# Five groups in the first tile list, tiles beside the last attention step, and 128 streamed columns in gates, values and logits

## What is computed

```python
q, k, v = layernorm(x), ctx, ctx                      # 32 x 128 x 256, 4 heads of 64
g = concat([q, k, v]) @ gate_kernel + bias            # input and forget gate of each head
cs = cumsum(log_sigmoid(fg)); log_D = tril(cs_i - cs_j) + ig_j
D = exp(log_D - max_j log_D); C = (q k^T / 8) * D
h = C / (max(|sum_j C|, exp(-max log_D)) + 1e-6) @ v
x = x + head_layernorm(h) * scale
n = layernorm(x); p = softmax(n @ router^T)           # 4096 tokens x 8 experts
top 2 of p, weights normalised
x = x + sum over the 2 experts e of w_e * (gelu(n @ w1[e]) @ w2[e])   # 256 -> 1024 -> 256
```

## Time and profile before

| | |
|---|---|
| median of 3 runs | 709.69 us |
| the profiled execution | 706.96 us, span of its instructions 705.2 us |
| PE matmul busy | 617.1 us (88%), 5872 records |
| PE weight load busy | 503.1 us (71%) |
| DVE, ACT, POOL busy | 402.6, 301.2, 253.3 us |
| mean granted TensorE clock | 0.846 |
| chain that ended last | PE 59%, DMA 12%, DVE 9%, issue 7% |

### The profile page before, as it was taken

One profiled execution on the slowest core, in us unless ns is written; L12 is line 12 of the kernel. 1 busy time (PEld: TensorE's weight loads), 2 busy tenths in 40 slices (PEclk: granted clock), 3 DMA queues, 4 the chain that ended last, 5 costly groups with the idle time before them and its releaser, 6 DMA issues.

```text
span 705.2 us, 18179 instructions
## 1 busy us (share of the span) xinstructions
PE 617.1 (88%) x5872; PEld 503.1 (71%) x5880; DVE 402.6 (57%) x1144; ACT 301.2 (43%) x583; POOL 253.3 (36%) x192
## 2 busy tenths in 40 slices
PE   2799989998899642999986999999999999999992
PEld 1577787786878541887765887888877787788781
DVE  1458688676876772655654555555555555455550
ACT  2444625616264210455423544445454445444441
POOL 0213237555474651153442222322221332232232
PEclk9965656557565555999998999999999999999997
DMA  9786485682832457164367326356489537438521
GB/s 313 281 317 218 181 300 206 243 309 81 299 152 82 187 191 287 36 169 116 75 199 202 63 45 164 53 140 189 96 261 284 142 53 234 95 49 296 148 38 22
DMA packets 56099, 120.18 MB, mean 170 GB/s; under 512 B 6064, under 2 KB 38064, under 8 KB 55024
## 3 DMA queue, kind: packets, MB, share of 16 engines
q1 hardware_dynamic: 40448, 99.37, 40.4%
q0 software_dynamic: 13392, 18.10, 14.6%
q10 hardware_dynamic: 2208, 2.11, 0.9%
HBM read 188.49 MB, written 40.13 MB: 324 GB/s over the span
## 4 chain that ended last, share of the span: by engine, by line
PE 59%; DMA 12%; DVE 9%; issue 7%; ACT 5%; POOL 3%; SPq 3%; ACTq 1%; POOLq 0%; DVEq 0%
PE bank L697 13%; PE bank L677 7%; PE bank L678 7%; PE bank L679 7%; PE bank L699 6%; DMA out<-yo,dst 6%; PE bank L600 6%; PE bank L528 4%; DMA wring<-wsplit 3%; PE bank L577 2%; PE bank L658 2%; PE bank L562 1%; DMA pad<-in_const_pad 1%; POOL rows L1438 1%; POOL hrs L1430 1%
## 5 line engine op out<-in xcount | busy, mean ns | idle before, releaser
L1465 POOL DMA_INDIRECT out<-yo,dst x71 | 114.2, 1609 | 292.1 <-DMA out<-yo,dst 167.9
L677 PE MATMUL bank<-wcv,wring 128*128 128x128 f16 x1136 | 200.4, 221 | 12.1 <-DVE wcv L1251 6.8
L678 PE MATMUL bank<-wcv,wring 128*128 128x128 f16 x1136 | 200.5, 221 | 0.0
L679 PE MATMUL bank<-wcv,wring 128*128 128x128 f16 x1136 | 200.4, 221 | 0.0
L1267 DVE TENSOR_TENSOR wcv<-wcv 128x512 f16<-128x512 f32 x142 | 98.3, 692 | 178.5 <-ACT wcv L881 121.0
L697 PE MATMUL bank<-wring,wcv 128*128 128x512 f16 x568 | 192.6, 380 | 1.1 <-DVE wcv L1267 1.1
L879 ACT ACTIVATE wcv<-bank 128x512 f32<-128x512 f32 x142 | 84.8, 597 | 213.1 <-PE bank L679 201.4
L699 PE MATMUL bank<-wring,wcv 128*128 128x256 f16 x568 | 155.0, 273 | 0.0
L677 PEld LDWEIGHTS bank<-wcv,wring 128*128 128x128 f16 x1136 | 112.2, 99 | 30.5 <-issue 15.4
L678 PEld LDWEIGHTS bank<-wcv,wring 128*128 128x128 f16 x1136 | 112.1, 99 | 1.5
L679 PEld LDWEIGHTS bank<-wcv,wring 128*128 128x128 f16 x1136 | 112.2, 99 | 0.0
(11 more groups left out here) (145 smaller groups left out, 803.1 us busy)
## 6 DMA issues: line engine op xcount, KB each, us to landing
wring<-wsplit SPq DMA_DIRECT2D x284, 512.0 KB
wring<-in_w SPq DMA_DIRECT2D x16, 1024.0 KB, 12.2
xrow<-rows SPq DMA_DIRECT2D x71, 130.0 KB
wsplit<-wring SPq DMA_DIRECT2D x4, 2048.0 KB, 7.9
wsplit<-wcv SPq DMA_DIRECT2D x4, 2048.0 KB, 7.9
xa<-in_x SPq DMA_DIRECT2D x8, 512.0 KB, 9.7
kT<-in_ctx_t SPq DMA_DIRECT2D x8, 512.0 KB, 8.4
ctn<-in_ctx SPq DMA_DIRECT2D x8, 512.0 KB, 8.2
```

Of the source, the lines that this page charges most:

```text
L677: pe.matmul(o, hi, xT[k][:, c, :], start=(c == 0), stop=False)
L678: pe.matmul(o, hi, xT[k][:, CK + c, :], start=False, stop=False)
L679: mm = pe.matmul(o, lo, xT[k][:, c, :], start=False, stop=(c == CK - 1))
L1465: pool.indirect_dma_start(out=out[:, :], out_offset=bass.IndirectOffsetOnAxis(ap=dst[o][:, 0:1], axis=0), in_=yo[o], in_offset=None, compu ...
```

## The change

Five things are edited.

- `gates`, `values` and `logits` stream 128 columns (`WIDE`) from where their operand starts: past their own 12, 66 or 8 columns come those of the next block, and behind the last block zeros. Only the first columns of each result are read; the next matmul writes over the rest. `vt` has 66 columns a head (two of ones), and the columns of `SB` are laid out anew, so that what is overwritten is not needed any more.
- `STAGES`: the first list is made in step 6 and has 33 tiles, those that groups 0 to 4 are sure to fill. `BEATS`: steps 7, 8 and 9 have 8 tiles each, 24 in all, where steps 8 and 9 had them. Three waits and bank choices that depend on `min(BEATS)` then hold for group 7: its values of batches 0 and 1 go to `SB`.
- `SPLIT`: experts 1 and 2 are both converted in step 0, and each later one a step earlier; step 6 has none.
- The list is cut into `list_counts`, `list_experts` and `list_rows`, with quarters of tiles and two operations of `head_var` between them.
- POOL's two stores of pad rows go from its start to the end of step 0.

```diff
-SPLIT = {e - 1: (e,) for e in range(NE)}
-BEATS = {8: 8, 9: 8}
-STAGES = {7: (0, 41), 9: (41, TILES)}
+SPLIT = {-1: (0,), 0: (1, 2), 1: (3,), 2: (4,), 3: (5,), 4: (6,), 5: (7,)}
+BEATS = {7: 8, 8: 8, 9: 8}
+STAGES = {6: (0, 33), 9: (33, TILES)}
...
+        gate_all = sb("gate_all", [P, 2 * CK * GC + WIDE])
+        gate_w = gate_all[:, 0:3 * CK * GC].rearrange("p (j n) -> p j n", j=3 * CK)
...
-        VO = 192
-        SF = SB[:, 0:G * GC]
-        CS = SB[:, 64:64 + R]
-        LG = SB[:, 96:96 + G * NE]
-        RK = SB[:, 128:128 + G * NE]
-        CN = SB[:, 160:160 + NE]
+        VO = 512 - (NH - 1) * VW - WIDE
+        CS = SB[:, 0:R]
+        RK = SB[:, 16:16 + G * NE]
+        CN = SB[:, 48:48 + NE]
+        LGO = 56
+        LG = SB[:, LGO:LGO + G * NE]
+        SFO = LGO + (G - 1) * NE + WIDE
+        SF = SB[:, SFO:SFO + G * GC]
...
-                        mm = pe.matmul(SF[:, b * GC:(b + 1) * GC], left, gate_w[:, j, :],
-                                       start=(j == 0), stop=(j == 2 * CK - 1))
+                        mm = pe.matmul(SB[:, SFO + b * GC:SFO + b * GC + WIDE], left,
+                                       gate_all[:, j * GC:j * GC + WIDE],
+                                       start=(j == 0), stop=(j == 2 * CK - 1), skip_group_check=True)
...
-                    mm = pe.matmul(o[:, h4 * (DH + 1):(h4 + 1) * (DH + 1)],
-                                   ct[b // 2][:, h4 % 2, c0:c0 + P], vt[g % 2][:, b, h4, :],
-                                   start=True, stop=True)
+                    v0 = (NH * b + h4) * VW
+                    mm = pe.matmul(o[:, h4 * VW:h4 * VW + WIDE], ct[b // 2][:, h4 % 2, c0:c0 + P],
+                                   vt_all[g % 2][:, v0:v0 + WIDE], start=True, stop=True, skip_group_check=True)
...
-                        mm = pe.matmul(LG[:, b * NE:(b + 1) * NE], rT[:, b, j, :], rwT[:, j, :],
-                                       start=(j == 0), stop=(j == CK - 1))
+                        mm = pe.matmul(SB[:, LGO + b * NE:LGO + b * NE + WIDE], rT[:, b, j, :],
+                                       rw_all[:, j * NE:j * NE + WIDE],
+                                       start=(j == 0), stop=(j == CK - 1), skip_group_check=True)
...
                 if T in STAGES:
-                    tile_list(T)
-                quarters(T, part, 14, 18)
+                    list_counts(T)
+                quarters(T, part, 14, 16)
+                if T in STAGES:
+                    list_experts(T)
+                quarters(T, part, 16, 18)
                 if_t(head_var, 0)
                 if_t(head_var, 1)
+                if T in STAGES:
+                    list_rows(T)
                 quarters(T, part, 18, 20)
...
                 quarters(T, part, 19, 32)
+                if T == 0:
+                    pad_spare()
```

More of the change, by code:

```diff
@@ L41 @@
 RING = 3
+VW = DH + 2
+WIDE = 128
 TILES = 2 * NT // P + NE - 1
@@ L116, in build @@
         pad = sb("pad", [P, ROW])
-        gate_w = sb("gate_w", [P, 3 * CK, GC])
+        gate_all = sb("gate_all", [P, 2 * CK * GC + WIDE])
+        gate_w = gate_all[:, 0:3 * CK * GC].rearrange("p (j n) -> p j n", j=3 * CK)
         gate_b = sb("gate_b", [P, G, GC])
         gam = sb("gam", [P, D])
-        rwT = sb("rwT", [P, CK, NE])
+        rw_all = sb("rw_all", [P, CK * NE + WIDE])
+        rwT = rw_all[:, 0:CK * NE].rearrange("p (j n) -> p j n", j=CK)
         mhalf = sb("mhalf", [P, R])
@@ L126, in build @@
         ctn = [sb(f"ctn{p}", [P, G, D]) for p in range(2)]
-        vt = [sb(f"vt{p}", [P, G, NH, DH + 1]) for p in range(2)]
+        vt_all = [sb(f"vt{p}", [P, R * VW + WIDE - VW]) for p in range(2)]
+        vt = [v[:, 0:R * VW].rearrange("p (b h d) -> p b h d", b=G, h=NH) for v in vt_all]
         st1 = sb("st1", [P, G, 6])
@@ L151, in build @@
         ct = [sb(f"ct{i}", [P, 2, 512]) for i in range(2)]
-        u = sb("u", [P, R, DH + 1])
+        u = sb("u", [P, R, VW])
         sq = sb("sq", [P, R, DH])
@@ L1196, in link, with listed, list_counts @@
                 dve.wait_ge(s_tb, link_at[0])
-            def tile_list(T):
+            def listed(T):
                 j0, j1 = STAGES[T]
-                n = j1 - j0
-                last = j1 == TILES
-                q_b = cst[:, C_TILE + j0:C_TILE + j1]
+                return j0, j1, j1 - j0, j1 == TILES, cst[:, C_TILE + j0:C_TILE + j1]
+            def list_counts(T):
+                j0, j1, n, last, q_b = listed(T)
                 dve.wait_ge(s_cnt, 1 + sorted(STAGES).index(T))
@@ L1217, in tile_list, with list_experts @@
                 link(dve.scalar_tensor_tensor(wt[:, :], av[:, :], -1.0, dd33[:, :], ALU.mult, ALU.add))
+            def list_experts(T):
+                j0, j1, n, last, q_b = listed(T)
                 link(dve.tensor_tensor(le[:, 0:n, :], q_b.unsqueeze(2).to_broadcast([P, n, NE]),
@@ L1223, in tile_list, with list_rows @@
                 link(dve.reduce_sum(adr[:, j0:j1], lw[:, 0:n, :], AX.X))
+            def list_rows(T):
+                j0, j1, n, last, q_b = listed(T)
                 link(dve.scalar_tensor_tensor(ad2[:, j0:j1], adr[:, j0:j1], done[:, 0:1], q_b, ALU.add, ALU.add))
@@ L1286, in _ @@
             x_stats(0)
+            dve.memset(gate_all[:, 3 * CK * GC:], 0.0)
+            dve.memset(rw_all[:, CK * NE:], 0.0)
             dve.memset(at[:, :, :], 0.0)
@@ L1397, in _ @@
             for p in range(2):
-                pool.memset(vt[p][:, :, :, DH:DH + 1], 1.0).then_inc(s_prepg, 1)
+                pool.memset(vt[p][:, :, :, DH:VW], 1.0).then_inc(s_prepg, 1)
+                pool.memset(vt_all[p][:, R * VW:], 0.0).then_inc(s_prepg, 1)
             pool.memset(mhalf[:, :], -0.5).then_inc(s_prepg, 2)
-            pool.wait_ge(s_prepg, 4)
+            pool.wait_ge(s_prepg, 6)
             def x_rstd(g):
@@ L1442, in _, with pad_spare @@
             x_rstd(0)
-            pool.wait_ge(s_prep, 16)
-            pool.dma_start(rows[SPARE:SPARE + P, :], pad[:, :]).then_inc(s_sc[0], 16)
-            pool.dma_start(out[NT:NT + P, :], pad[:, 0:D]).then_inc(s_sc[1], 16)
+            def pad_spare():
+                pool.wait_ge(s_prep, 16)
+                pool.dma_start(rows[SPARE:SPARE + P, :], pad[:, :]).then_inc(s_sc[0], 16)
+                pool.dma_start(out[NT:NT + P, :], pad[:, 0:D]).then_inc(s_sc[1], 16)
             stored = [0]
```

2 lines of the change are left out of this document (1 added, 1 removed).

## The result

The changed kernel takes 682.95 us (median of 4 runs, 680.79 to 684.54) against 711.41 us for the kernel before (4 runs, 704.34 to 715.73): ratio 0.964, 95% interval 0.9592 to 0.9688. The prediction was 687.0 us. In every comparison the ratio is taken without executions that are more than 1.5% above the fastest of their kernel, the medians with them. The profiled execution took 682.88 us, its span is 681.1 us. It ran 24.1 us shorter than the span before, and two numbers divide that: the first tile starts at 240.56 instead of 277.50 (36.9 earlier), and from there to the end it takes 440.5 us instead of 427.7 (12.9 longer).

A forecast was written before the change was run, and what follows sets the result against it. It took TensorE, busy but mostly at its lower clock, as bounding the attention steps, beside a chain through three engines. Tile 0 at 244.1 plus 439.7 gave a span of 683.8, so 685.6 profiled; predicted 687 us, range 672 to 700.

The forecast's parts named there:

- The price of a wide record: In the attention steps, a float32 record of 128 columns takes 0.251 us slow, 0.136 fast; a slow-clock step grows 2 us.
- Start and step 0: Ahead of step 1: nothing booked for the start; step 0's own values gain 1.4 us.
- The double conversion: Two experts converted in step 0: step 1's last values end at 76.5 instead of 75.24, + 1.3 us.
- Steps 2 to 6: Attention steps with wide matmuls save 10.8 us together, between 7.8 and 14.8.
- gates near 4.4 us: Sign of being right in steps 2 to 6: gates near 4.4 us, with a granted clock above 0.8.
- E: Time E: end of step 6's last values; rival E: weight load and streaming add up, about 820 us, chance 0.05.
- What holds tile 0: Before the first tile: rows' load goes out behind the experts' weight loads, scatters don't hold it; tile 0 at 244.1.
- From tile 0 on: From tile 0 to the end: 427.7 us becomes 439.7, with step 7's values, wide logits and stalls added.
- rival D: Tiles beside step 7 stall; if waits cost 15 us more, 702 us; chance 0.11.
- most of it at the start of step 8: Sign of being right: tile 0 to the end takes 11 to 12 us more, mostly at step 8's start, priced at 5.
- B: Rival: the clock does not help, or rises only where DVE is awaited; change - 10.6, 697 us; chance 0.17.
- C: Rival: steps shrink to DVE's work, 25 us a step; five steps save 23.7 us; 673 us; chance 0.12.

The follow-up runs named there:

- e1: Changed kernel with gates, values and logits back at 12, 66 and 8 streamed columns; 704.62 us, ratio 0.9958 to the kernel before.
- e2: Changed kernel with SPLIT, BEATS and STAGES of the kernel before, so the wide columns nearly alone; 690.22 us, ratio 0.9749.
- e3: Changed kernel with experts 6 and 7 converted together in step 5 instead of 1 and 2 in step 0; 683.40 us, ratio 0.965.
- e7: Changed kernel with POOL's last two scatters of the listed group ahead of head_rstd in step 6; 681.45 us, ratio 0.9622.
- e4: Changed kernel with step 7's four groups of values and their copies ahead of the first tile; 678.83 us, ratio 0.9607.

## Why the prediction was right, point by point

**What bounds it: right.** TensorE busy at a low clock was the diagnosis, and it is confirmed by taking the columns away (e1: clock 0.84 and 704.6) and by adding them alone (e2: 0.926 and 690.2). The total came out closer than its parts would have it, which is partly luck: step 1 ends 4.2 us earlier than forecast, steps 2 to 6 give back 1.8 of that, and behind tile 0 two errors cancel (below). The last step of the sum isn't derived either: its own terms give 685.6 for a profiled execution and 688.3 for the median, and 687 stands between them.

**The price of a wide record: wrong, and too high.** I took 0.251 us slow and 0.136 fast from the scores, which use half the array's rows. Full-height records measured 0.214 and 0.112 for gates. Eight values records start 1.71 us before the next matmul when slow (182.56 to 184.27 in step 5) and 0.89 when fast (43.45 to 44.34 in step 0), 0.214 and 0.111 each. The 0.246 that I read from the earlier trace rows for values of 65 columns is a recorded length, not a pitch: the last eight of that step in the kernel before stand 1.61 us ahead of the next matmul (193.87 to 195.48), 0.201 each. So of the 2 us a step that I booked for a low clock about half a microsecond exists at most. The Trainium skill, TensorE: Matmul & The Clock Gate, says in its section on packing small matmuls that a weight load overlaps matmuls in flight only where the row group differs. The gates don't bear that out: all their loads are full-height, and the pitch is the same with 12 and with 128 columns.

**Start and step 0: undersized.** I gave nothing for the start and 1.4 us for step 0. Group 0's gates rise to the high level after 2.7 us (in the timeline before they stayed low for all of their 7 us), so attention starts 1.75 us earlier, and step 0 is 3.3 shorter (18.68 against 22.02): 5.1 in all. I had looked for the gain only from step 2 on.

**The double conversion: about right as a length.** I had step 1 last 27.3 us (49.2 to 76.5), and it lasted 26.8. It ended at 72.3 because it began 3.7 us earlier and was 0.5 shorter. Against the same kernel with single conversions it costs 3.6 us (e3).

**Steps 2 to 6: 9.0 us saved, 10.8 forecast,** within its bounds of 7.8 to 14.8. The account held in the main: the slow front parts of steps 4 and 5 shrank, the steps evened out at 27 to 29 us, DVE is awaited in them, and the clock, 0.80 to 0.88, is not full. Of the 5.2 us that step 4 lost, 2.7 lie ahead of the gates, 0.3 in them and 2.2 behind. But the sign "gates near 4.4 us" failed: they take 5.3 to 6.6 us in these steps, since half of their records or more run at the low level, behind a wait of TensorE of 1.3 to 2.0 us.

**Step 6's end at 211.9 (214.4), table 217.7 (221), tile 0 240.6 (244.1).** From E on, the list took 5.8 instead of 6.7 and the first tile came after 28.6 instead of 29.7.

**What holds tile 0: wrong in its cause.** I wrote that the scatters "don't hold it" and that the rows' load goes out behind the weights. The earlier trace rows already said otherwise of the kernel before: the last scatter lands at 271.45 (265.41 + 6.04), the weights' issues end at 265.91, and the rows' load goes out at 272.26. So I read a wait for the scatters as a wait for the queue. The chain of the changed kernel shows the same, by two steps that I had not weighed: POOL issues its last two scatters behind `head_rstd`, 2.93 us, and this waits for `head_var`, the end of which stands behind the list. The number came out because the last scatter landed 16.1 us after the table where it had been 17.0, and because the two branches are nearly equal: without the scatters the load goes out 3.6 us earlier and lands 1.1 us earlier (e7). A right price was no proof of its cause.

**From tile 0 on: 12.9 us more, 12 forecast.** TensorE's stall at the start of step 8 is 3.79 us before the matmul at 302.43, where I had 5. No other gap of TensorE over 0.3 us stands between 243 and 352, so step 7 itself stalls less than the 1.5 I set; rival D fell with it. The sum behind the 12.9 was wrong in both halves:

```profile
277.50:705.10 427.60, 400.48 (x4721) 322.56 (x4721) 221.01 (x622) 191.18 (x360) 130.78 (x87) 0.97 0.51 131
240.56:681.00 440.44, 410.85 (x4782) 332.52 (x4782) 231.02 (x666) 197.04 (x373) 142.96 (x98) 0.96 0.50 126
```

The first row is the kernel before, the second the changed one. TensorE's busy time grew by 10.4 us, where I had 6.5 for moved work and wide logits; its idle time grew by 2.5, where I had 5.5 (stalls of 6.5 less 1 from the list). e4 takes 4.4 back by moving the values ahead. That the other part of the busy time comes from the slightly lower clock is likely, and not shown. The sign "most of it at the start of step 8" failed: that stall is 3.8 of the 12.9.

**The rivals.** B (the clock doesn't help) is refuted by e2. C asked for steps of 25 us; they are 26.9 to 29.0 at a mean clock of 0.85, and none of the experiments reaches 25 in steps 3 to 6. E rested on load and stream adding up, which the pitch of 0.214 us refutes.

**What I missed.** The stretch between the last two rows, 363.30 to 379.30, holds the pad stores' gap. I wrote "ACT's pad stores remain" and asked no further; spreading them was worth as much (7.6 us) as list, tiles and conversions on top of the wide columns (7.3).

## What to carry to other kernels

Read the granted clock beside the busy time: an engine busy for 96% of a step may be at half speed. Where matmuls of few columns keep their pitch with more, as the gates here did, columns that nobody reads can pay for themselves: compare the pitch at both widths, and the granted clock. Here it took all three kinds of matmul to bring steps 2 to 6 from a clock of 0.57 to 0.85; gates alone reached 0.66. When a load goes out late, compare its time with the end of each thing it could wait for, before pricing the wait. After an edit at one place, list every gap of the bounding engine above half a microsecond, before and after: the best single gain here was a gap that neither kernel had been questioned about.

## What was not expected of the hardware

- A float32 record with a full-height weight load has the same pitch with 12 and with 128 columns: 0.214 us at 1.2 GHz, 0.112 at 2.4 GHz.
- Widening gates alone and values alone saved 4.1 and 3.2 us in steps 2 to 6, both with the logits 14.0 (one profile each).
- Eight small stores in a row on ACT's queue took 7.95 us and kept ACT from its work for 8.54; one alone took 0.34.
- The rows of the last indirect scatter landed 5.96 us after its issue, and the load of rows took 5.89 us with SyncE's weight loads ended 5 us before it, 8.43 us when it followed them by 0.9 us. (In the first case they had ended at 229.2, the load went out at 234.6.)
- On two chips, TensorE had stretches of 8 to 10 us in each step with tiles in which it paused every 0.7 us or so with nothing awaited; the kernel before took 730 us there against about 710 on the other chips. Their cause is open.
